# Attention with a third key stack buffer, a reordered opening, and work moved into the last groups

## The reference

```
# 1 attention, 16 heads of 32 columns, keys = values = ctx (4 x 2048 x 512)
q = layernorm(x) * s; k = ctx * s; w = softmax(q k^T)
x = x + (w ctx) @ w_proj.T + b_proj
# 2 gated scan over the tokens (norm, W_in, tanh, sigmoid, scan, W_out)
# 3 mixture of experts: 8 experts of 512, 2 for each token, and 2 shared ones
```

## Time and profile before

| what | value |
|---|---|
| median of 3 runs | 536.14 us (534.79 to 537.72) |
| profiled execution, its own time | 541.33 us |
| its span, first to last instruction | 539.5 us |
| PE busy / DVE busy / ACT busy / POOL busy | 471.8 / 398.6 / 330.7 / 293.7 us |
| mean granted TensorE clock | 0.978 |
| mean DMA rate | 248 GB/s |

### The profile page before, as it was taken

The page is one execution under the profiler, slowest core; times in us unless marked ns, Lnnn a source line. Parts: engine busy times, 40 slices in busy tenths (PEclk is TensorE's granted clock), DMA queues, the critical chain, the costliest instruction groups (busy, mean ns, idle before and its releaser), DMA issues.

```text
span 539.5 us, 15770 instructions
## 1 busy us (share of the span) xinstructions
PE 471.8 (87%) x6731; PEld 330.4 (61%) x6731; DVE 398.6 (74%) x603; ACT 330.7 (61%) x361; POOL 293.7 (54%) x278
## 2 busy tenths in 40 slices
PE   0478998899997979999999955999999999999995
PEld 0135666666665656676667542854788787887642
DVE  2577776687775767877771799588599999999426
ACT  4245776577675766767555373367478898888320
POOL 2338898999997996999769440373001011010032
PEclk9999999999999998999999996799999999999998
DMA  8598987979979698777698721065999999998125
GB/s 266 110 267 279 254 239 185 230 226 251 258 204 261 157 258 229 230 198 180 139 391 331 293 88 68 1 197 213 421 382 398 417 416 418 416 416 348 40 77 176
DMA packets 48249, 133.94 MB, mean 248 GB/s; under 512 B 6450, under 2 KB 31282, under 8 KB 37426
## 3 DMA queue, kind: packets, MB, share of 16 engines
q1 hardware_dynamic: 44500, 120.88, 69.5%
q0 software_dynamic: 3680, 12.06, 6.1%
HBM read 96.74 MB, written 11.01 MB: 200 GB/s over the span
## 4 chain that ended last, share of the span: by engine, by line
PE 45%; DVE 35%; issue 8%; DMA 6%; POOL 2%; ACT 2%; SPq 1%; DVEq 0%; ACTq 0%; POOLq 0%
DVE mx L699 11%; DVE ws L773 10%; PE bank L1024 8%; PE bank L989 8%; PE bank L1033 7%; PE bank L1009 6%; DMA kt<-in_keysT 4%; DMA wst<-in_ffw 3%; DVE rden L716 2%; PE bank L1147 2%; PE bank L1148 2%; PE bank L1149 2%; DVE hf L914 2%; DVE hl L919 2%; PE bank L1090 1%
## 5 line engine op out<-in xcount | busy, mean ns | idle before, releaser
L699 DVE TENSOR_REDUCE mx<-bank 128x1 f32<-128x512 f32 x256 | 163.1, 686 | 71.2 <-PE bank L989 70.4
L458 ACT ACTIVATE pt<-bank 128x1024 f32<-128x1024 f32 x128 | 125.9, 1023 | 71.1 <-PE bank L1009 71.1
L617 POOL TENSOR_TENSOR ps<-pt 128x512 f32<-128x512 f32 x128 | 160.1, 1280 | 10.9 <-PE bank L1033 5.7
L989 PE MATMUL bank<-kstk,q 96*128 96x512 f16 x256 | 96.9, 410 | 29.2 <-issue 8.7
L773 DVE SCALAR_TENSOR_TENSOR ws<-wst,ws 128x2048 f16<-128x2048 f32 x51 | 115.5, 2287 | 2.0 <-ACT ws L502 1.8
L502 ACT ACTIVATE ws<-wst 128x2048 f16<-128x2048 f32 x48 | 90.5, 1904 | 4.6 <-DMA wst<-in_ffw 4.5
L590 POOL TENSOR_TENSOR kl<-kt,kh 128x512 f16<-128x512 f32 x62 | 70.7, 1166 | 24.9 <-ACT kh L423 24.9
L1009 PEld LDWEIGHTS bank<-q,kstk 98*128 98x128 f16 x1024 | 68.2, 100 | 23.3 <-issue 4.8
L1162 PE MATMUL bank<-xt,ws 128*128 128x128 f16 x480 | 81.2, 219 | 0.8 <-DVE hf L914 0.8
L1009 PE MATMUL bank<-q,kstk 98*128 98x128 f16 x1024 | 80.3, 223 | 1.7 <-ACT pt L458 1.0
L1164 PE MATMUL bank<-xt,ws 128*128 128x128 f16 x480 | 81.2, 219 | 0.0
(11 more groups left out here) (162 smaller groups left out, 628.5 us busy)
## 6 DMA issues: line engine op xcount, KB each, us to landing
wst<-in_ffw SPq DMA_DIRECT2D x51, 1024.0 KB, 11.2
kt<-in_keysT SPq DMA_DIRECT2D x16, 1024.0 KB, 6.1
kstk<-kh SPq DMA_DIRECT2D x128, 128.0 KB, 3.4
v<-in_vals SPq DMA_DIRECT2D x16, 1024.0 KB, 9.0
kstk<-kl SPq DMA_DIRECT2D x64, 128.0 KB, 3.8
xs_rows<-biases SPq DMA_DIRECT2D x15, 256.0 KB, 3.0
x_tok<-xs_rows POOLq DMA_DIRECT2D x15, 256.0 KB, 8.4
ys_rows<-xn POOLq DMA_DIRECT2D x15, 256.0 KB, 6.6
```

Source lines behind the costliest of these rows:

```text
L458: act.activation(pt[:, n % 4, :, :, :].rearrange("p j a t -> p (j a t)"), bank[:, 2 * (n % 2):2 * (n % 2) + 2, :].rearrange("p j n -> p (j ...
L617: pool.tensor_tensor(ps2[:, n % 4, :, :], pt[:, n % 4, 0, :, :], pt[:, n % 4, 1, :, :], ALU.add)\
L699: dve.tensor_reduce(mx[:, a, q:q + 1], bank[:, 4 + k % 2, :], AX.X, ALU.max).then_inc(m_taken, 1)
L989: pe.matmul(bank[:, 4 + k % 2, :], q1[:, j % 2, a, :], kstk[0:KS, j % 2, a, q * 512:(q + 1) * 512], start=True, stop=True).then_inc(m_read ...
```

## The change

- There is a third stack, `third`, laid into the part of `wst` that holds the second set of feed-forward weights. SP now stacks group i+3 in its loop for i, first the high rows (after ACT's split) and then the low rows (after POOL's), and waits for the scores of group j-3. The constants are issued after the loop of i = 12, the first three weight loads after i = 13, the other three when all scores of group 14 are done.
- Opening: the other batches of `x` are loaded when keys 0 have arrived, keys 1 after the copies of stack 0. ACT issues four of the copies itself. The low parts of keys 0 and 2 are made by VectorE for three of four heads. ACT copies the queries before it splits keys 1; keys 2 are split in group 0, keys 3 later in group 0. The 16 maxima of group 0 use six banks and are reduced two banks at a time. Two scores come before the first maxima of group 1. The other batches are scaled in groups 1, 5 and 9. Small activations load ACT's tables ahead of need.
- Last groups: POOL adds the bias in groups 13 and 14, after sums 2 and 5, each waiting for all constants. In group 15 VectorE makes the pair sums, and between them scales `win`, makes the constants and splits the first weights' low part. ACT splits two of the first weights in group 14, and the third after group 15. POOL's residual adds all wait for VectorE's last `xn`.

```diff
+    third = wst[0:KM, 1, :, :, :].rearrange("p m c n -> p (m c n)").bitcast(F16)[:, 0:HG * S]
+    stacks = [kstk[:, 0, :, :], kstk[:, 1, :, :], third.rearrange("p (a s) -> p a s", a=HG)]
...
         def stack(j, h):
+            sp.wait_ge(split_hi, 2 * j + 2)
+            if j >= 3:
+                sp.wait_ge(st_done, HS * (j - 3) + HS // 2 * (h + 1))
+            copies(j, h, kh, (0, 2 * HD))
             sp.wait_ge(split_lo, j + 1)
-            if j >= 2:
-                sp.wait_ge(st_done, HS * (j - 2) + HS // 2 * (h + 1))
-            copies(j, h, kh, (0, 2 * HD))
+            if j == 2:
+                sp.wait_ge(lo_dve, 4)
             copies(j, h, kl, (HD,))
...
+        sp.wait_ge(kt_in[0], 16)
         sp.dma_start(x[:, 1:B, :], t["x"][:, 1:B, :]).then_inc(x_in, 16)
-        load_k(1)
         sp.wait_ge(split_hi, 2)
         copies(0, 0, kh, (0, 2 * HD))
-        sp.wait_ge(lo_dve, 1)
+        sp.wait_ge(lo_dve, 2)
         sp.wait_ge(split_lo, 1)
         copies(0, 0, kl, (HD,))
-        stack(0, 1)
+        copies(0, 1, kl, (HD,))
+        load_k(1)
+        load_v(0)
         stack(1, 0)
         load_k(2)
-        load_v(0)
         stack(1, 1)
         load_k(3)
+        load_v(1)
+        stack(2, 0)
+        stack(2, 1)
         for i in range(G):
             if i + 4 < G:
                 load_k(i + 4)
-            if i + 1 < G:
+            if 0 < i < G - 1:
                 load_v(i + 1)
-            if i + 2 < G:
-                stack(i + 2, 0)
-                stack(i + 2, 1)
-            if i == G - 3:
+            if i + 3 < G:
+                stack(i + 3, 0)
+                stack(i + 3, 1)
+            if i == G - 4:
                 for dst, name in CONSTS:
                     sp.dma_start(dst, t[name]).then_inc(consts, 16)
-            if i == G - 2:
-                for u in range(2):
-                    for m in range(3):
-                        sp.dma_start(wst[:, u, m, :, :], t["ffw"][2 * u, m]).then_inc(w_in[u][m], 16)
+            if i == G - 3:
+                for m in range(3):
+                    sp.dma_start(wst[:, 0, m, :, :], t["ffw"][0, m]).then_inc(w_in[0][m], 16)
+        sp.wait_ge(st_done, HS * (G - 1))
+        for m in range(3):
+            sp.dma_start(wst[:, 1, m, :, :], t["ffw"][2, m]).then_inc(w_in[1][m], 16)
...
(ACT, before the loop over the groups)
+        act.wait_ge(eps_set, 2)
+        act.activation(r1[:, 0, 0:2], eps[:, :], ACT.Sqrt)
         for h in range(2):
             split_keys(0, h)
-        act.wait_ge(eps_set, 2)
         root(ln1_var, 1, 0, 1)
+        act.wait_ge(split_hi, 2)
+        stack_rows(act, 0, 1, kh, (0, 2 * HD))
         queries_high(0)
         queries_high(1)
+        take_queries(0)
+        take_queries(1)
+        root(ln1_var, B, 1, B)
+        act.activation(r1[:, 1, 0:2], eps[:, :], ACT.Exp)
         for h in range(2):
             split_keys(1, h)
-        root(ln1_var, B, 1, B)
-        take_queries(0)
-        take_queries(1)
-        for h in range(2):
-            split_keys(2, h)
...
(ACT, in the loop)
+                if i == G - 2 and p in (0, 2):
+                    split_first(p // 2)
                 if p == 1 and i + 2 < G:
                     take_queries(i + 2)
-                if p < 2 and i + 3 < G:
-                    split_keys(i + 3, p)
+                if i == 0 and p < 2:
+                    split_keys(2, p)
+                if p in ((2, 3) if i == 0 else (0, 1)) and i + 3 < G:
+                    split_keys(i + 3, p % 2)
...
(POOL)
-        for i in range(G):
+            pool.wait_ge(xn_done, B)
+            pool.wait_ge(consts, NC)
+            pool.tensor_tensor(x[:, b, :], x[:, b, :], bproj[:, :], ALU.add).then_inc(xb_done, 1)
+        for i in range(G - 1):
             for hs in range(HS):
                 pair_sum(HS * i + hs)
+                if i == 0 and hs == 4:
+                    split_keys(2, HG - 1)
+                if hs in ((5, 7) if i == 0 else (3, 5)) and i + 3 < G:
+                    for a in ((0, 1) if hs == (5 if i == 0 else 3) else (2, 3)):
                         split_keys(i + 3, a)
+                if i in (G - 3, G - 2) and hs in (2, 5):
+                    add_bias(2 * (i - G + 3) + hs // 3)
-        add_bias()
         pool.wait_ge(xb_done, B)
         pool.memset(zero[:, :], 0.0).then_inc(zero_set, 1)
+        pool.wait_ge(h_done, B)
...
(DVE)
+        for k in range(0, MB, 2):
+            a, q = block_of(k)
+            dve.wait_ge(m_ready, k + 2)
+            pair = 2 * (k // 2 % 3)
+            dve.tensor_reduce(mx[:, a, q:q + 2], bank[:, pair:pair + 2, :], AX.X, ALU.max).then_inc(m_taken, 2)
...
         for i in range(G):
             for p in range(HS // 2):
                 for j, k in maxima_in(i, p):
                     take_max(j, k)
+                if i == G - 1:
+                    pair_sum(HS * i + 2 * p)
+                    pair_sum(HS * i + 2 * p + 1)
                 if p == 0 and i > 0:
                     invert(i - 1)
                     divide(i - 1)
+                if p == 1 and i in (1, 5, 9):
+                    first_normed(i // C + 1)
                 if p == 2 and i + 1 < G:
                     shift(i + 1)
+                if i == G - 1 and p == 0:
+                    scale_win()
+                if i == G - 1 and p == 1:
+                    make_constants()
+                if i == G - 1 and p == 2:
+                    split_low(0, 0)
+                if p in (1, 2) and i == 0:
+                    low_parts(2, p - 1)
         invert(G - 1)
         divide(G - 1)
+        split_low(0, 1)
...
(PE)
-        first_products(-1, 3)
+        pe.wait_ge(ones_in, 32)
+        scores(0)
+        scores(1)
+        for j, k in maxima_in(-1, 3):
+            max_scores(j, k)
```

More of the change, by code:

```diff
@@ L200, in build_program @@
     x0_in = sem("x_first_batch_loaded")
-    id_in = sem("identity_and_ones_loaded")
+    id_in = sem("identity_loaded")
+    ones_in = sem("ones_rows_loaded")
     kt_in = [sem("kt_loaded_0"), sem("kt_loaded_1")]
     v_in = [sem("v_loaded_0"), sem("v_loaded_1")]
-    k_rep = [[sem(f"k_stacked_{q}_{h}") for h in range(2)] for q in range(2)]
+    k_rep = [[sem(f"k_stacked_{q}_{h}") for h in range(2)] for q in range(3)]
     split_hi = sem("split_hi")
@@ L318, in build_program, with stack_rows @@
     blk = block.__enter__()
+    def stack_rows(eng, j, h, src, rows):
+        for row in rows:
+            for q in (2 * h, 2 * h + 1):
+                eng.dma_start(stacks[j % 3][row:row + HD, :, q * S // 4:(q + 1) * S // 4],
+                              src[q * HD:(q + 1) * HD, j % 2, :, :]).then_inc(k_rep[j % 3][h], 16)
     @blk.sync
@@ L421, in split_keys @@
                     for half in range(2):
[L422 removed]
+                        act.wait_ge(k_rep[(j - 2) % 3][half], 16 * 6 * ((j - 2) // 3 + 1))
             act.activation(kh[:, j % 2, heads, :].rearrange("p a s -> p (a s)"),
@@ L478, in _, with split_first @@
         queries_high(2)
+        def split_first(m):
+            act.wait_ge(w_in[0][m], 16)
+            if m == 0:
+                act.wait_ge(split_lo, G)
+                for j in (G - 2, G - 1):
+                    for half in range(2):
+                        act.wait_ge(k_rep[j % 3][half], 16 * 6 * (j // 3 + 1))
+            act.activation(ws[:, 0, 0, m, :, :].rearrange("p c n -> p (c n)"),
+                           wst[:, 0, m, :, :].rearrange("p c n -> p (c n)"), ACT.Copy, scale=WS).then_inc(w_hi[m], 1)
         for i in range(G):
@@ L514, in copy_normed @@
                            ACT.Copy).then_inc(hnT_act, 1)
+        split_first(2)
+        act.wait_ge(consts, NC)
+        act.activation(wo[:, 0, :], wout[:, :], ACT.Copy, scale=WS).then_inc(wo_hi, 1)
         for b in range(B):
@@ L602, in queries_low @@
             pool.tensor_tensor(z[:, :, 2 * HD:KS], q, z[:, :, 0:HD], ALU.subtract).then_inc(xs_lo, 1)
-        for a in range(2, HG):
-            split_keys(0, a)
+        split_keys(0, HG - 1)
         queries_low(0)
         queries_low(1)
-        for j in range(1, 3):
-            for a in range(HG):
-                split_keys(j, a)
+        for a in range(HG):
+            split_keys(1, a)
         queries_low(2)
@@ L741, in _ @@
         first_norm(1, B)
-        for k in range(MB):
-            take_max(0, k)
+        for k in range(0, MB, 2):
[3 more added lines that the diff above has]
+            dve.tensor_reduce(mx[:, a, q:q + 2], bank[:, pair:pair + 2, :], AX.X, ALU.max).then_inc(m_taken, 2)
         shift(0)
@@ L755, in scale_win @@
                     .then_inc(win_done, 1)
-        for i in range(G):
-            if i == G - 1:
-                scale_win()
-            for p in range(HS // 2):
-                for j, k in maxima_in(i, p):
-                    take_max(j, k)
-                if p == 0 and i > 0:
-                    invert(i - 1)
-                    divide(i - 1)
-                if p == 2 and i + 1 < G:
-                    shift(i + 1)
```

(34 more changed lines are left out.)

83 lines of the change are left out of this document (32 added, 51 removed).

## The result

The changed kernel takes **551.2 us** (median of 4 runs, 546.08 to 552.11) where the kernel before took 535.46 in the same comparison (4 runs, 530.42 to 537.72): ratio **1.027, 95% interval 1.021 to 1.033**, slower. The forecast was 534.7 with a range of 525 to 541. The profiled execution took 550.63 us, with a span of 548.8 and a mean granted clock of 0.960, against 541.33, 539.5 and 0.978.

The account below looks back on a forecast made before the run. No engine bounds everywhere; in undisturbed 15.19 us groups PE and POOL are nearly full, and stack waits lose 11.6 us. Terms sum to -4.0, giving 537.3 profiled, then 534.7 after half of the 5.2 above the median; range 525 to 541.

Parts of the forecast that it names:

- The third stack: Attention groups: copies issued a whole group earlier remove PE's stalls before the maxima, -11.6 us, taken whole.
- rival D: Attention groups: DMA is the limit, value loads come late and half of the 11.6 stays, 540.5 us; chance 0.08.
- I split it in half: Whole run: half of the profiled execution's 5.2 us above the median counted as removed stack waits, 537.3 to 534.7.
- The opening: Start through first groups: earlier first maxima, gain mostly taken back by later keys; 0 us, bounds -5 to +5.
- maxima from about 16: Opening: stack 0 issued until 13 plus 3.5 to land, so PE's first maxima start at about 16 us, before 21.39.
- rival B: PE at group 2's first maxima: opening ends slower, losing if first values end after 42.5; +5, 539.7 us; chance 0.12.
- +1.5: Group 1: POOL about 2.4 us behind its pace after the moved split of keys 3, catching up 0.46 a group.
- The bias: Group 13: POOL waits 9 us for the last constant, PE stalls 7; +7 us, bounds 0 to +9.
- Norm and scan: After the projection: 3.2 us to win at the scan's start, less slowing by POOL's adds; -1.8, bounds -3.2 to +2.
- Rival C: Scan: shared port lock makes eight operations, instead of three, pay 0.7 to 1.2 us each; +5, 539.7 us; chance 0.10.
- two or three of the scan's operations pay that, 0.7 each: Scan on VectorE: only two or three operations slowed beside POOL's adds, 0.7 us each.
- Feed-forward: Feed-forward stage: one 2.28 us low part leaves VectorE's queue where PE is full; -0.9 us, bounds 0 to -2.3.

Follow-up runs that it names:

- Run 2: Kernel before with only the third key stack and its order of copies, constants and weight loads; old opening and end: 532.04 us, ratio 0.987.
- Run 11: Changed kernel with the projection bias issued first among the constants on its own semaphore, bias additions waiting for that alone: 538.34 us, ratio 1.005.
- Run 5: Changed kernel with keys 2 loaded right behind keys 1 and split before group 0, keys 3 split at the usual place: 538.15 us, ratio 1.000.
- Run 8: Changed kernel with keys 2 early, bias adds after group 14's sums, residual adds not held, plus first low part moved behind the last sums: 524.21 us, ratio 0.971.
- run 9: Changed kernel, keys 2 early, residual adds not held; group 15's pair sums on POOL, two bias adds in group 14, two after those sums: 527.54 us, ratio 0.983.
- run 3: Changed kernel without POOL's wait for the last scaled copy, so its adds run beside the projection: 543.13 us, ratio 1.013.
- run 1: Changed kernel with POOL's bias additions moved from groups 13 and 14 to behind its sums of group 14: 541.57 us, ratio 1.008.

## Why the prediction was wrong

**The third stack: right in the trace, wrong as a term of the median.** All windows from 5 to 12 are at 15.19, and so rival D doesn't hold there. But the step "I split it in half" failed. The changed kernel's profiled execution stands 0.6 below its median, so nothing of the 5.2 was left to subtract; 3.2 of the 16.5 us by which I missed are this: 2.6 counted on, and those 0.6. Run 2 is worth 5.7 us in medians. That the 5.2 were stack waits, as I wrote, isn't shown, since only one execution of the kernel before was profiled.

**The opening: the largest miss, 8.6 us (3.0 + 5.6 against 0).** Three steps failed.

The first is "maxima from about 16". Four issues on ACT took 2.72 us and the low copies were issued until 15.13 on SP, so the last rows landed at 20.6; I took 13 for the issue and 3.5 for the landing, where it was 5.5. (The price of 1.2 us a pair of banks was right: 9.14 us in all.) The load of keys 1 took longer as well: issued at 15.17, it let ACT split at 23.71, 8.5 us later, while the numbers that I wrote down for that chain leave 5.4 for it, without saying so. The first values ended at 43.1 instead of 41 and the maxima of group 2 came at 55.41 instead of 53.5, 1.9 us late. The 12.5 us between these two held (12.3), and this is rival B's case, just past its limit of 42.5.

The second is the price of the stall. PE's wait before those maxima was 3.00 us where I had 4, but I gave the slow matmuls behind it nothing, and they cost 2.6 up to the first reciprocal. Run 11 shows the same wait without them.

The third is "+1.5" for POOL, where groups 1 to 4 lost 5.6. The split of keys 3 waited 6.04 us for ACT (row 63.43), whose part stood behind exponentials that PE released late. Its last two quarters, with four pair sums queued behind them, ran from there on; then POOL had group 4's split too and no gap: it is busy 17.10 of 17.10 in group 1. The value load of group 2 stands behind the half stacks of group 3 on SP's queue: it is issued at 73.85, where the kernel before issued it at 58.16, and lands 8.9 us later, at 82.7. PE's first values of group 2 begin at 82.81, after 1.06 us without work; the row names ACT's exponentials, but these were done before. The value load of group 3, issued at 86.12, takes 12.9 us. Groups 2 and 3 stay over the pace.

Run 5 shows that one edit is behind all of this: with keys 2 split in time there is no stall, no fall of the clock and no late load, and 10.5 us are back. How much POOL's queue, the value loads and the clock each cost in groups 1 to 4 was not separated; in run 11, whose clock didn't fall, these groups lost 2.6 instead of 5.6.

**The bias: the wait exact, its echo not.** 7 us were forecast and 7.01 measured; the last issue came at 259.7 instead of 262 and POOL's three sums ended 3 us earlier too. The mis-sized term is the clock. I had the row that showed it (the group of the 2.48 stall cost 1.8 more than its stall, clock 0.91) and used it only as an upper bound of 9. After 7 us without work it was 3.0, with the window at 0.80. The price doesn't simply follow the length of the stall: it was 1.8 after 2.48 us, and in the opening 2.6 or nothing after the same 3.00.

**ACT's splits in group 14: +0.2 for +1; group 15: +1.8 for +2.3.** Right in kind. Run 8 shows that the low part is what stretches group 15 and that moving it gives nothing; run 9 shows that with the preparations there the group is longer when POOL has the sums.

**Norm and scan: +1.2 for -1.8.** Rival C, to which I gave 0.10. The failed step is "two or three of the scan's operations pay that, 0.7 each". The 3.2 us "to win" were there: the scan began 4.4 us earlier after the last reciprocal than before, and in run 3 the first `scan_y` follows it by 27.2 us instead of 30.8. But six operations paid, 5.5 us in all, and the four scans most. The condition I wrote myself, that POOL's eight additions outlast the start of the scan "which they do", is an argument that the rival happens, and its chance should have been set by it. The Trainium skill (SBUF — State Buffer, the section on the two separate sides) says that whichever of the two engines has the pair of ports keeps it for the whole instruction and that VectorE operations with two SBUF inputs are concerned; each scan has two, and took 1.37 to 1.41 us, about the 1.27 of one of POOL's additions. By that rule alone eight waits were the price, which is nearer to the six found than my two or three, and the trace agrees for these. `scan_a`, which has one such input, paid too (0.42 to 0.99), so two inputs aren't the whole condition here.

**Feed-forward: -0.9 for -0.9.** No run shows this term by itself, and the match can be luck: in run 2, whose end is that of the kernel before, the stretch from `scan_y` on took 213.9 us, less than the 214.8 of the changed kernel.

The terms together: -11.6 + 8.6 + 10.0 + 0.2 + 1.8 + 1.2 - 0.9 = +9.3, the measured difference of the profiled executions, against -4.0 forecast. Of the 13.3 between them 8.6 are the opening, 2.6 of them its clock, 3.0 the clock after the stall in group 13 and 3.0 the scan, less 1.3 on the two groups. For the clock and the scan the trace of before had shown the mechanism, and I took a price near its cheap end or none; for the opening no row showed the landing under the new load.

## What to carry to other kernels

A wait moved into a loop in which two engines are full must be for exactly the transfer that is needed: one semaphore for twelve loads made 10 us out of an edit that costs nothing with its own. Price a stall of a matrix engine with the slow matmuls behind it, and work that is moved "off the path" with whoever shares a port or a queue there. When a profiled execution lies above the median, don't count on any of that excess being left after a change that removes stalls: the gain of this one, 11.6 us in the trace, was 5.7 in medians. And read a loss in more than one execution: the same opening cost 4 us more or less from one to the next.

## What the runs showed of the hardware

- A VectorE operation that reads SBUF (the memory that the engines work in), beside running POOL additions, often takes about as long as one of them, however small it is: 128x8 elements took 1.25 us against 0.17, a conversion of 128x32 elements 1.25 against 0.17, a scan over 128x128 1.37 to 1.41 against 0.40 to 0.42. POOL pays as well: four additions took 7.69 us beside VectorE, against 4.95 for four in the earlier trace rows. Not each one pays: the scan at 277.60 in run 9 kept its 0.41, and VectorE's maxima, which read PSUM, took 0.68 to 0.69 us each in group 1 of the changed kernel with POOL busy throughout.
- The clock after a stall: 2.48 us of idle PE went with a window at 0.91, 7.01 us with one at 0.80 and 3.0 us of lost time; 32 value matmuls took 1.93 us behind it and 1.06 otherwise. An idle 3.00 us in the opening went with 0.50 from 55.4 to 61.0 in the changed kernel, and with 1.00 in run 11.
- DMA shares of 0.98 and 1.00 in group 13 (runs 1 and 11) left it at 15.20 and 15.19 us: full queues cost that group nothing. In group 2 of the changed kernel, at 1.10, a late value load cost PE 1.06 us.
